# Lambda-layer kernel: one q load moved to ScalarE's queue, weight slots interleaved with the last output tiles, loads of the next x tied to TensorE's slots

## The chip, the cores and the metric

One core of one Trainium2 chip. The metric is the device time of one launch in microseconds, for a batch of 32 images. Less is better.

## The reference

For each of 32 images (512 channels, 64 x 64 pixels, float32), with n = group normalization of x over 32 groups:

```
h   = relu(bn1(conv1x1(n, w1)))                     # 512 -> 128 channels
q   = bnq(conv1x1(h, q_w))                          # 4 heads x 16
k   = softmax over the 16 of conv1x1(h, k_w)
v   = bnv(conv1x1(h, v_w))                          # 32 channels
content = k v^T over all pixels                     # 16 x 32
pos     = conv 15x15 of v with emb (16 kernels)     # 16 x 32 per pixel
out = q . (content + pos)                           # 4 heads x 32 = 128
out = bn3(conv1x1(relu(bn2(out)), w3))              # 128 -> 512
result = x + relu(out + n)
```

## The kernel before

**Tiling.** An image is 4 chunks (j) of 1024 pixels. X holds a chunk as 128 partitions x 4 channel tiles (t) x 1024. The 16 output tiles are called oj.t, tile number 4j + t. PSUM is a ring of four tiles of 128 x 1024 (ring 0 to 3); each named step of TensorE takes one, by a fixed table (`placed`), and waits until the step that had it before has been moved out.

**Stages of an image.** The loop over images has two stages on every engine, and each engine runs through its own list in order.

- `lam(b)`: the position part of image b. The 15 x 15 window is treated as six units u. For each unit TensorE first makes eight weight slots w{u}.{s} (L508: q times the expanded emb, 4 matmuls of 256 columns), which ScalarE or VectorE copy from the ring to `region` (L702; the table BY_DVE says which are VectorE's), and then multiplies them with windows of v (L653). The slots run one unit ahead: while unit u is multiplied, w{u+1}.* are made. At units 0 and 3 a content product (L607) starts the sums in rings 2 and 3; the sums of units 0 to 2 are copied out to S (L711) before the content product of unit 3 may begin. Units 1 and 4 add a small rest (L617). In the same stage VectorE takes the group statistics of the next image's x (L884, 32 instructions, four to each half chunk), placed between its slots by STATS_AT: chunk 0 in unit 1 from slot 4 on, ten statistics in unit 2 of which the last two are of chunk 2, the rest in unit 3. The mean and variance products (L545, L547) follow in unit 4.
- mixed stage, order list MIX: conv1 (c0 to c3, L527), q and k/v (L534, L539) of image b + 1, the content sums (cl, L555; cp, L559), the 16 output tiles of image b (L583), and the slots of unit 0 of image b + 1 with the rest r0, r1 (L517). Of the output tiles nine go VectorE (L1031, into one of four buffers T), ScalarE (relu, L741), GpSimd (addition into X, L1189); the other seven are VectorE's alone in two instructions (L1035, L1038). bcur, rcur and r1cur, which these use, are overwritten by VectorE at the end of the stage.

**Where the data goes.** SP issues nearly all transfers, in order: q's parts go to DRAM and come back in another layout (store_q, load_q: L353, L354, L360, six DMAs of 128 KB to a chunk), v likewise as windows (store_v L367, L370; load_v L377, L378, 3 x 1024 KB; load_v3 L384, 672 + 336 KB into the place of the first, once unit 0 is done). store_out is L402 (512 KB each), load_x L345 (2048 KB a chunk, after all stores out of that chunk of X are done), shuffle L389 and L393 (the sums to DRAM and back as h2). ScalarE issues the reload of x for the residual (L788), one chunk after each conv1.

SP's order in a loop step: load_x 0 to 3, load_v3, the two shuffles, then q chunk 0, stores 0 and 1, q chunk 1, store 2, q chunk 2's store, store 3, q chunk 3's store, load_q 2, load_q 3, store_v, stores 4 to 7, load_v, stores 8 to 15. TensorE waits for all four q_in before w0.0.

The order at the end of MIX before:

```
... cl o2.0 cp o2.1 o2.2 o2.3 o3.0 w0.0 o3.1 w0.1 o3.2 w0.2 o3.3 w0.3 w0.4 w0.5 w0.6 w0.7 r0 r1
```

Of the kernel before, what the change touches and what calls it, by code (L numbers as in the profile page):

```python
# [17 lines left out]
CHUNK = 1024  # L18
# [4 lines left out]
SPLIT = [(0, 0), (0, 1), (0, 2), (1, 0), (1, 1), (2, 0)]  # L23
NG = len(SPLIT)
# [7 lines left out]
UNITS = 6  # L32
# [3 lines left out]
NS = 8  # L36
GUARD = 8


BY_DVE = {0: (5, 7), 1: (1, 3, 5), 2: (1, 3), 3: (3,), 4: (3,), 5: (1, 3, 5, 7)}  # L40
ACT_SLOTS = [(u, s) for u in range(UNITS) for s in range(NS) if s not in BY_DVE[u]]
DVE_SLOTS = [(u, s) for u in range(UNITS) for s in range(NS) if s in BY_DVE[u]]

STATS_AT = {1: (0, 0, 0, 0, 2, 2, 2, 2), 2: (1, 1, 1, 2, 1, 1, 2, 1), 3: (2, 2, 2, 2, 2, 2, 2, 0)}


VEC_TILES = [0, 2, 3, 6, 9, 12, 15]
POOL_TILES = [n for n in range(16) if n not in VEC_TILES]
NVEC, NPOOL = len(VEC_TILES), len(POOL_TILES)
# [5 lines left out]


def lead_names():
    return [f"w0.{s}" for s in range(NS)] + ["r0", "r1"]


def mix_names():
    order = ["c0", "nb", "c1", "q0", "k0", "o0.0", "o0.1", "c2", "q1", "k1", "o0.2", "o0.3", "c3", "q2", "k2", "q3", "k3",
             "o1.0", "o1.1", "o1.2", "o1.3", "cl", "o2.0", "cp", "o2.1", "o2.2", "o2.3"]
    lead = lead_names()
    for t in range(4):
        order += [f"o3.{t}", lead[t]]
    return order + lead[4:]


def lam_names():  # L70
# [3 lines left out]
def placed(order, first=0):  # L74


    out, n = {}, first
    for name in order:
        if name[0] == "w":
            out[name] = int(name[3:]) % 2  # L80
        elif name[0] == "r":
            out[name] = int(name[1])
        elif name in ("gm", "gv"):
            out[name] = 1
        elif name.startswith("o3"):
            out[name] = 2 + int(name[3:]) % 2
        elif name == "cp":
            out[name] = out["cl"]
        else:
            out[name] = n % 4  # L90
            n += 1
    return out


def lambda_block(nc, x, w1, bn1, wq, bnq, wk, wv, bnv, emb, bn2, w3, bn3, out):
    B, C, H, W = x.shape
    N = H * W
# [3 lines left out]
    DK = wk.shape[0]  # L101
    DV = wv.shape[0]
    HEADS = QC // DK
    KV = DV + DK
    NCH = N // CHUNK
# [15 lines left out]
    with ctx:  # L121
# [3 lines left out]
        def sem(name):  # L125
            return ctx.enter_context(nc.semaphore(name))
# [3 lines left out]
        Qt = sb("Qt", [P, HEADS * N], BF16)  # L130
# [36 lines left out]
        qD = nc.dram_tensor("q_parts", (QC, NPART, N), BF16, kind="Internal").ap()  # L167
# [13 lines left out]
        o1 = 8192  # L181
# [6 lines left out]
        r1 = region[QC:2 * QC, o1 + 6144:o1 + 8192].rearrange("p (u n) -> p u n", u=2)  # L188
# [33 lines left out]
        w_full = sem("w_full")  # L222
# [44 lines left out]
        half_relu = sem("half_relu")  # L267
# [2 lines left out]

        x_in = [sem(f"x_in{j}") for j in range(NCH)]
        res_in = [sem(f"res_in{j}") for j in range(NCH)]
        out_done = [sem(f"out_done{j}") for j in range(NCH)]
        q_out = [sem(f"q_out{j}") for j in range(NCH)]
        q_in = [sem(f"q_in{j}") for j in range(NCH)]
# [44 lines left out]
                holds[at[name]] = name  # L320
            return out

        LAST_LEAD = {0: "r0", 1: "r1"}
        BEFORE_PRO = prior(PRO, AT_PRO, {})
        BEFORE_LAM = prior(LAM, AT_LAM, LAST_LEAD)
        BEFORE_LAM_END = prior(LAM_END, AT_LAM_END, LAST_LEAD)
# [16 lines left out]
        def _(sp):  # L343
            def load_x(im, j):
                sp.dma_start(X[:, j, :, :], xv[im, :, :, j * CHUNK:(j + 1) * CHUNK]).then_inc(x_in[j], 16)  # L345
# [10 lines left out]
            def load_q(im, j):  # L356
                sp.wait_ge(q_out[j], im * 32 + 32)
                for g, (a, _e) in enumerate(SPLIT):
                    dst = bass.AP(Qt, g * (HEADS * N) + j * CHUNK, [[NG * HEADS * N, DK], [N, HEADS], [1, CHUNK]])
                    sp.dma_start(dst, qD[:, a, j * CHUNK:(j + 1) * CHUNK].rearrange("(h k) n -> k h n", k=DK))\  # L360
                        .then_inc(q_in[j], 16)
# [18 lines left out]
            def load_v3(b):  # L380
                sp.wait_ge(first_done, b + 1)
                for p0, n, col in ((0, 84, 18), (84, 42, 4)):
                    src = bass.AP(vD.tensor, col * WROWS * ROW, [[ROW, n], [BLK * WROWS * ROW, NXB], [1, ROW]])
                    sp.dma_start(V[p0:p0 + n, 0, :, :], src).then_inc(v_in[3], 16)  # L384
# [28 lines left out]
            for g in range(NG):  # L413
                dst = bass.AP(region, g * 16384 + emb_at, [[NG * 16384, DK], [1, RR]])
# [14 lines left out]
            for x0 in (0, PAD + W):  # L429
                for a in range(0, WROWS, BLK):  # L430
                    n = min(BLK, WROWS - a)
# [11 lines left out]
            def lam(b, last):  # L443
                if not last:
                    for j in range(NCH):
                        sp.wait_ge(out_done[j], b * (16 * CT) + HEAD)
                        load_x(b + 1, j)
                load_v3(b)
                shuffle(b, 0)
                shuffle(b, 1)  # L450

            with nc.Fori(0, B - 1, engines=OrderedEngineSet([sp.engine]), hint_back_edge=True,
                         head_slot={sp.engine: 0}) as b:
                lam(b, False)
                store_q(b + 1, 0)
                load_q(b + 1, 0)
                store_out(b, 0)
                store_out(b, 1)
                store_q(b + 1, 1)
                load_q(b + 1, 1)  # L460
                store_out(b, 2)
                store_q(b + 1, 2)
                store_out(b, 3)
                store_q(b + 1, 3)
                load_q(b + 1, 2)
                load_q(b + 1, 3)
                store_v(b + 1)
                for n in range(4, 8):
                    store_out(b, n)
                load_v(b + 1)  # L470
                for n in range(8, 16):
                    store_out(b, n)
            e = B - 1
            for j in range(NCH):
# [240 lines left out]
        def _(act):  # L715
# [86 lines left out]
            def lead(name, at, im):  # L802
# [4 lines left out]
                elif (0, int(name[3:])) in ACT_SLOTS:  # L807
                    slot(at[name], im, 0, int(name[3:]))

            def keys_out(at, im):  # L810
                act.wait_ge(cl_full, im + 1)
                nc.scalar.copy(clS, ring[at["cl"]][96:96 + DK, 0:DV]).then_inc(cl_ready, 1)
# [16 lines left out]
            with nc.Fori(0, B - 1, engines=OrderedEngineSet([act.engine]), hint_back_edge=True,  # L829
                         head_slot={act.engine: 0}) as b:  # L830
                lam(b, True)
                late = []
                for name in MIX:
                    if name[0] in "wr":
                        lead(name, AT_MIX, b + 1)
                    elif name == "cl":
                        keys_out(AT_MIX, b + 1)
                    elif name[0] in "cqk" and name[1] in "0123":
                        front(name, AT_MIX, b + 1, True)
                    for n in late:  # L840
                        relu_half(b, n)
                    late = []
                    if name == "c0":
                        bn2_relu(b, 0)
                        bn2_relu(b, 1)
                    if name == "k0":
                        bn2_relu(b, 2)
                        bn2_relu(b, 3)
                    if name[0] == "o" and int(name[1]) * CT + int(name[3:]) in POOL_TILES:
                        late.append(int(name[1]) * CT + int(name[3:]))  # L850
                assert not late
# [8 lines left out]
        def _(dve):  # L860
# [58 lines left out]
            def keep_for_output(chain):  # L919
                chain(nc.vector.tensor_copy(rcur[:, :], rstd[:, :]))  # L920
                chain(nc.vector.tensor_scalar(r1cur[:, :], rstd[:, :], 1.0, None, ALU.add))
                chain(nc.vector.tensor_copy(bcur[:, :], bnew[:, :]))
# [128 lines left out]
            def mixed(chain, order, at, b, im):  # L1051
                for name in order:
                    if name[0] in "wr":
                        lead(name, at, im)
                    elif name[0] == "o":
                        output(chain, name, at, b)
                    elif name == "nb":
                        gn_bias(at, im)
                    elif name == "cp":
                        content(chain, name, at, im)  # L1060
                    elif name[0] in "qk":
                        front(chain, name, at, im)
                        if name == "k3":
                            softmax_sum(chain, im, NCH - 1)
# [9 lines left out]
            g, be, m, v = (par[:, a, :] for a in range(4))  # L1074
# [23 lines left out]
            for i, rows in ((0, R), (1, R - 1)):  # L1098
                dst = Ep[:, i, GUARD + 3 * WROWS:GUARD + (3 + R) * WROWS].rearrange("p (b a) -> p b a", a=WROWS)
# [25 lines left out]
            with nc.Fori(0, B - 1, engines=OrderedEngineSet([dve.engine]), hint_back_edge=True,  # L1125
                         head_slot={dve.engine: 0}) as b:
                chain = Chain(b * LOOP_LINKS + pre)
                lam(chain, b, True)
                mixed(chain, MIX, AT_MIX, b, b + 1)
                keep_for_output(chain)  # L1130
                assert chain.n == LOOP_LINKS, chain.n
            chain = Chain((B - 1) * LOOP_LINKS + pre)
# [116 lines left out]
```

## Time and profile before

| | |
|---|---|
| runs of the kernel before | 4826.49, 4826.06, 4821.62 us, median 4826.06 |
| the profiled execution | 4817.23 us, its span 4815.5 us |
| TensorE busy (matmul) | 4457.8 us, 93% |
| VectorE, ScalarE, GpSimd busy | 2796.9, 2346.0, 967.9 us |
| mean granted clock of TensorE | 0.949 |
| moved by DMA | 1284.17 MB, mean 267 GB/s |

The busy time of an engine says how much it did, not what held the end. In the chain of waits, time goes to what released the next step. A granted clock of 1.00 is 2.4 GHz and 0.50 is 1.2 GHz. The DMA share is the mean busy share of the 16 DMA engines; it can come out a little over 1. All rows of the loop below are of one image, from 1972 to 2119 us, and the begin of the next.

### The profile page before, as it was taken

How to read it: one execution, taken by the hardware profiler on the slowest of the kernel's cores; microseconds unless marked ns; L12 is line 12 of the kernel's file. 1: busy time of each engine (PE TensorE's matmuls, PEld its weight loads, DVE VectorE, ACT ScalarE, POOL GpSimd, SP SyncE). 2: the span in 40 equal slices, each digit the busy share in tenths (PEclk: the TensorE clock that was granted, in tenths of full speed). 3: DMA queues.
4: the chain of work that ended last, by engine and by line, in shares of the span. 5: the costliest groups of instructions: out<-in, count | busy, mean ns of one | idle time of the engine just before them, and what ended most of it. 6: DMA issues, size and time to landing. Idle time of an engine off the chain costs nothing.

```text
span 4815.5 us, 121009 instructions
## 1 busy us (share of the span) xinstructions
PE 4457.8 (93%) x49366; PEld 2717.4 (56%) x49366; DVE 2796.9 (58%) x4631; ACT 2346.0 (49%) x2880; POOL 967.9 (20%) x529
## 2 busy tenths in 40 slices
PE   4899999999999999999999999999999999999997
PEld 2555565655556655555555555555565556555555
DVE  3465555565655665656656556556566565566564
ACT  1455445554545454445544454544455444545453
POOL 0022211122201222202222112222122221112221
PEclk9899999999999999999999999999999999999998
DMA  3689778888778897788887788977888878889877
GB/s 96 214 278 308 239 265 279 275 296 277 249 272 266 282 309 250 254 274 288 281 291 243 265 266 276 307 251 254 272 292 281 288 245 275 270 273 305 263 248 250
DMA packets 537174, 1284.17 MB, mean 267 GB/s; under 512 B 43048, under 2 KB 225324, under 8 KB 528556
## 3 DMA queue, kind: packets, MB, share of 16 engines
q1 hardware_dynamic: 471276, 1017.22, 65.7%
q10 hardware_dynamic: 65472, 260.05, 14.7%
q8 instruction: 416, 6.82, 0.6%
q14 instruction: 10, 0.08, 0.0%
HBM read 844.79 MB, written 432.33 MB: 265 GB/s over the span
## 4 chain that ended last, share of the span: by engine, by line
PE 45%; SPq 18%; DMA 13%; issue 11%; DVE 6%; POOL 4%; ACT 2%; ACTq 0%; POOLq 0%; DVEq 0%
PE ring L527 16%; DMA X<-x_dram 11%; PE ring L653 10%; PE ring L508 7%; SPq L402 5%; PE ring L583 4%; SPq L360 4%; DVE st L884 3%; DMA q_parts<-region 3%; SPq L377 3%; POOL X L1189 2%; PE ring L534 2%; POOL region L1182 2%; SPq L378 2%; PE ring L539 2%
## 5 line engine op out<-in xcount | busy, mean ns | idle before, releaser
L702 ACT COPY region<-ring 126x1024 f32<-126x1024 f32 x1120 | 1102.9, 1016 | 948.0 <-PE ring L508 934.0
L583 PE MATMUL ring<-h,w3T 128*128 128x512 f32 x2048 | 937.7, 601 | 28.6 <-DVE X L1038 15.3
L653 PE MATMUL ring<-region,V 126*32 126x128 f32 x24576 | 889.2, 289 | 42.9 <-issue 42.7
L527 PE MATMUL ring<-X,w1e 128*128 128x512 f32 x2048 | 907.7, 596 | 3.2 <-DVE w1e L910 3.2
L508 PE MATMUL ring<-Qt,Ep 96*126 96x256 bf16 x5120 | 808.3, 298 | 103.9 <-DVE region L702 52.0
L653 PEld LDWEIGHTS ring<-region,V 126*32 126x32 f32 x24576 | 692.0, 116 | 223.3 <-issue 206.8
L702 DVE COPY region<-ring 126x1024 f32<-126x1024 f32 x416 | 507.5, 1220 | 496.6 <-PE ring L508 496.5
L508 PEld LDWEIGHTS ring<-Qt,Ep 96*126 96x126 bf16 x5120 | 598.9, 146 | 323.1 <-issue 139.4
L884 DVE BATCH_NORM_STATS2 st<-X 128x6 f32<-128x512 f32 x1024 | 624.8, 679 | 198.0 <-DMA X<-x_dram 197.9
L527 PEld LDWEIGHTS ring<-X,w1e 128*128 128x128 f32 x2048 | 384.5, 190 | 468.8 <-issue 465.5
L583 PEld LDWEIGHTS ring<-h,w3T 128*128 128x128 f32 x2048 | 370.0, 190 | 410.9 <-issue 371.5
L993 DVE SCALAR_TENSOR_TENSOR region<-ring,pbi,region 64x512 f32<-64x512 f32 x256 | 179.5, 739 | 723.8 <-ACT region L794 722.8
L1182 POOL TENSOR_TENSOR region<-region 64x1024 bf16<-64x1024 f32 x128 | 273.5, 2137 | 1177.6 <-ACT region L798 1177.6
L1189 POOL TENSOR_TENSOR X<-X,S 128x1024 f32<-128x1024 f32 x160 | 377.5, 2359 | 481.9 <-ACT S L741 481.9
L786 ACT ACTIVATE region<-ring,nb 128x1024 f32<-128x1024 f32 x128 | 142.5, 1113 | 625.8 <-PE ring L527 352.2
L1175 POOL MEMSET region<- 64x224 f32 x32 | 9.1, 284 | 2170.4 <-PE ring L653 2126.8
L1035 DVE SCALAR_TENSOR_TENSOR ring<-X,r1cur,ring 128x1024 f32<-128x1024 f32 x224 | 287.2, 1282 | 40.8 <-PE ring L583 40.8
L1189 POOL TENSOR_TENSOR X<-X,region 128x1024 f32<-128x1024 f32 x128 | 302.5, 2363 | 11.8 <-ACT region L741 7.9
L539 PEld LDWEIGHTS ring<-wkvT,region 128*128 128x128 f32 x2048 | 238.2, 191 | 103.8 <-issue 77.9
L1038 DVE SCALAR_TENSOR_TENSOR X<-ring,bcur,X 128x1024 f32<-128x1024 f32 x224 | 287.7, 1284 | 8.0
L741 ACT ACTIVATE S<-S,bcur 128x1024 f32<-128x1024 f32 x160 | 183.5, 1147 | 202.3 <-DVE S L1031 200.9
L539 PE MATMUL ring<-wkvT,region 128*128 128x48 f32 x2048 | 254.1, 277 | 0.0
(130 smaller groups left out, 3317.4 us busy)
## 6 DMA issues: line engine op xcount, KB each, us to landing
X<-x_dram SPq DMA_DIRECT2D x132, 2048.0 KB, 20.1
out_dram<-X SPq DMA_DIRECT2D x512, 512.0 KB, 8.0
X<-x_dram ACTq DMA_DIRECT2D x124, 2048.0 KB, 10.6
Qt<-q_parts SPq DMA_DIRECT2D x768, 128.0 KB, 3.1
V<-v_windows SPq DMA_DIRECT2D x96, 1024.0 KB, 10.5
lambda_sums<-S SPq DMA_DIRECT2D x64, 1024.0 KB, 5.0
h<-lambda_sums SPq DMA_DIRECT2D x256, 256.0 KB, 5.0
q_parts<-region SPq DMA_DIRECT2D x128, 256.0 KB, 4.2
```

The lines of the kernel that those rows point to most:

```text
L402: sp.dma_start(ov[b, :, t, j * CHUNK:(j + 1) * CHUNK], X[:, j, t, :]).then_inc(out_done[j], 16)
L508: last = nc.tensor.matmul(dst[0:TROWS, i * 256:(i + 1) * 256], taps(u, xo, yo), Q[:, :, xo * BLK + yo, :], start=(i % 2 == 0), stop=True, ...
L527: last = nc.tensor.matmul(dst[:, hh * HALF:(hh + 1) * HALF], w1e[:, c, :], X[:, j, c, hh * HALF:(hh + 1) * HALF], start=(c == 0), stop=(c ...
L539: last = nc.tensor.matmul(dst[:, i * KV:(i + 1) * KV], h1[:, j % 2, i * P:(i + 1) * P], wkvT[:, :], start=True, stop=True)
L583: last = nc.tensor.matmul(dst[:, yb * HALF:(yb + 1) * HALF], w3T[:, t, :], src, start=True, stop=True)
L653: last = nc.tensor.matmul(bank_of(i)[c * DV:(c + 1) * DV, (g % 4) * P:(g % 4 + 1) * P], V[0:TROWS, VSLOT[t], xb, yb * DV:(yb + 1) * DV], W ...
L702: return engine_copy(dst, src)
L884: return nc.vector.bn_stats(st[:, c, 2 * j + hh, :], X[:, j, c, hh * HALF:(hh + 1) * HALF])
L1035: nc.vector.scalar_tensor_tensor(src[:, :], X[:, j, t, :], r1cur[:, t:t + 1], src[:, :], ALU.mult, ALU.add).then_inc(whole_sum, 1)
L1038: nc.vector.scalar_tensor_tensor(X[:, j, t, :], src[:, :], bcur[:, t:t + 1], X[:, j, t, :], ALU.add, ALU.max).then_inc(out_ready, 1)
L1182: nc.gpsimd.tensor_tensor(q12[:, 1, cols], r1[:, j % 2, :], q12[:, 0, cols], ALU.subtract)\
L1189: nc.gpsimd.tensor_tensor(X[:, j, t, :], X[:, j, t, :], T[i % 4], ALU.add).then_inc(pool_out, 1)
```

## The change

- The last q chunk's six loads move from SP to ScalarE's queue, behind its copy of the content sums `cl`. ScalarE waits there for q_out[3].
- MIX is reordered: slots w0.0 and w0.1 go behind o2.2 and o2.3, and two steps (w0.2 and w0.3; r0 and r1; w0.4 and w0.5; w0.6 and w0.7) go behind each of o3.0 to o3.3. o2.2 and o2.3 take ring 2 and 3. VectorE's slots of unit 0 are 3 and 5 instead of 5 and 7.
- load_x(1), (2) and (3) wait until TensorE has finished 8, 14 and 20 slots of lam (w1.7, w2.5, w3.3). load_v3 stands behind load_x(1) instead of behind load_x(3). x_turn is counted up around the wait and nothing waits for it.
- store_out(7) goes behind load_v.
- VectorE waits for ScalarE's last relu of the image before it overwrites bcur.

The order at the end of MIX after:

```
... cl o2.0 cp o2.1 o2.2 w0.0 o2.3 w0.1 o3.0 w0.2 w0.3 o3.1 r0 r1 o3.2 w0.4 w0.5 o3.3 w0.6 w0.7
```

```diff
-BY_DVE = {0: (5, 7), 1: (1, 3, 5), 2: (1, 3), 3: (3,), 4: (3,), 5: (1, 3, 5, 7)}
+BY_DVE = {0: (3, 5), 1: (1, 3, 5), 2: (1, 3), 3: (3,), 4: (3,), 5: (1, 3, 5, 7)}
+X_AFTER = [0, 8, 14, 20]
 def lead_names():
-    return [f"w0.{s}" for s in range(NS)] + ["r0", "r1"]
+    return ["w0.0", "w0.1", "w0.2", "w0.3", "r0", "r1", "w0.4", "w0.5", "w0.6", "w0.7"]
 def mix_names():
...
-             "o1.0", "o1.1", "o1.2", "o1.3", "cl", "o2.0", "cp", "o2.1", "o2.2", "o2.3"]
-    lead = lead_names()
+             "o1.0", "o1.1", "o1.2", "o1.3", "cl", "o2.0", "cp", "o2.1", "o2.2", "w0.0", "o2.3", "w0.1"]
+    lead = lead_names()[2:]
     for t in range(4):
-        order += [f"o3.{t}", lead[t]]
-    return order + lead[4:]
+        order += [f"o3.{t}", lead[2 * t], lead[2 * t + 1]]
+    return order
...
-        elif name.startswith("o3"):
+        elif name.startswith("o3") or name in ("o2.2", "o2.3"):
             out[name] = 2 + int(name[3:]) % 2
...
-        LAST_LEAD = {0: "r0", 1: "r1"}
+        LAST_LEAD = {0: "w0.6", 1: "w0.7"}
...
                     for j in range(NCH):
                         sp.wait_ge(out_done[j], b * (16 * CT) + HEAD)
+                        if j:
+                            sp.sem_inc(x_turn, 1)
+                            sp.wait_ge(w_full, b * (UNITS * NS) + NS + X_AFTER[j])
+                            sp.sem_inc(x_turn, 1)
                         load_x(b + 1, j)
-                load_v3(b)
+                        if j == 1:
+                            load_v3(b)
+                else:
+                    load_v3(b)
                 shuffle(b, 0)
...
                 load_q(b + 1, 2)
-                load_q(b + 1, 3)
                 store_v(b + 1)
-                for n in range(4, 8):
+                for n in range(4, 7):
                     store_out(b, n)
                 load_v(b + 1)
-                for n in range(8, 16):
+                for n in range(7, 16):
...
+            def load_q(im, j):
+                act.wait_ge(q_out[j], im * 32 + 32)
+                for g, (a, _e) in enumerate(SPLIT):
+                    dst = bass.AP(Qt, g * (HEADS * N) + j * CHUNK, [[NG * HEADS * N, DK], [N, HEADS], [1, CHUNK]])
+                    act.dma_start(dst, qD[:, a, j * CHUNK:(j + 1) * CHUNK].rearrange("(h k) n -> k h n", k=DK))\
+                        .then_inc(q_in[j], 16)
...
                         keys_out(AT_MIX, b + 1)
+                        load_q(b + 1, NCH - 1)
...
                 mixed(chain, MIX, AT_MIX, b, b + 1)
+                dve.wait_ge(half_relu, b * NPOOL + NPOOL)
                 keep_for_output(chain)
```

## Rows read from the trace of the kernel before

**Rows 1.** The page: busy time of the engines, and DMA queue q1.

```profile
PE 4457.8 (93%) x49366; PEld 2717.4 (56%) x49366; DVE 2796.9 (58%) x4631; ACT 2346.0 (49%) x2880; POOL 967.9 (20%) x529
...
q1 hardware_dynamic: 471276, 1017.22, 65.7%
```

**Rows 2.** The chain that ended last: start us, us, what.

```profile
1972.03 7.06 PE ring L527 x16
...
2065.52 19.62 DMA X<-x_dram
...
2119.18 7.06 PE ring L527 x16
```

**Rows 3.** Timeline of TensorE: start us, us, instruction, count [idle before <-releaser].

```profile
2049.64 0.65 PE L508 MATMUL ring<-Qt,Ep 96*126 96x256 bf16 x4 [0.67 <-ACT region L702]
...
2053.91 1.03 PE L517 MATMUL ring<-Qt,E 96*22 96x256 bf16 x4 [0.78 <-DVE region L702]
...
2057.30 3.60 PE L607 MATMUL ring<-Qt,CLp 96*32 96x512 bf16 x16
...
2077.72 0.36 PE L617 MATMUL ring<-Qt 22*32 22x16 f32 x20 [1.21 <-issue]
...
2088.22 0.65 PE L508 MATMUL ring<-Qt,Ep 96*126 96x256 bf16 x4 [1.09 <-DVE region L702]
...
2093.66 1.90 PE L607 MATMUL ring<-Qt,CLp 96*32 96x512 bf16 x16 [0.53 <-DVE S L711]
```

**Rows 4.** Timeline of VectorE: the statistics in lam, then tile 9's last step.

```profile
2080.09 4.84 DVE L884 BATCH_NORM_STATS2 st<-X 128x6 f32<-128x512 f32 x8 [5.96 <-DMA X<-x_dram]
2085.17 1.88 DVE L884 BATCH_NORM_STATS2 st<-X 128x6 f32<-128x512 f32 x3 [0.23 <-DMA X<-x_dram]
...
2091.05 1.87 DVE L884 BATCH_NORM_STATS2 st<-X 128x6 f32<-128x512 f32 x3
...
2184.87 1.28 DVE L1038 SCALAR_TENSOR_TENSOR X<-ring,bcur,X 128x1024 f32<-128x1024 f32 x1
```

**Rows 5.** Windows: stretch, length, busy by engine (count), PEclk, DMA share, GB/s.

```profile
2030.00:2045.00 15.00, 14.49 (x92) 7.55 (x89) 14.75 (x17) 8.31 (x9) 12.91 (x6) 1.00 0.79 201
2045.00:2062.00 17.00, 14.28 (x91) 7.58 (x93) 9.28 (x11) 9.71 (x10) 5.83 (x3) 0.74 1.03 338
2092.00:2097.00 5.00, 4.47 (x62) 2.76 (x62) 5.00 (x9) 2.75 (x4) 0.00 (x0) 1.00 1.04 231
2049.00:2054.00 5.00, 2.58 (x17) 1.61 (x18) 4.07 (x4) 3.36 (x4) 2.04 (x1) 0.92 1.01 326
2053.50:2063.50 10.00, 9.31 (x65) 5.00 (x66) 3.32 (x6) 3.17 (x4) 0.00 (x0) 0.50 1.07 354
```

**Rows 6.** Timeline of SP's queue: issue of q loads 2 and 3, and of V3.

```profile
2030.13 7.61 SPq L360 DMA_DIRECT2D Qt<-q_parts  x12
...
2076.09 13.17 SPq L384 DMA_DIRECT2D V<-v_windows  x2
```

**Rows 7.** ScalarE's copy of the keys; tile Qt, 2170 to 2200: q loads and landing.

```profile
2178.83 0.18 ACT L812 COPY Qt<-ring 16x32 f32<-16x32 f32 x1
2181.36 1.15 ACT L741 ACTIVATE region<-region,bcur 128x1024 f32<-128x1024 f32 x1 [2.36 <-DVE region L1031]
...
L360 SPq DMA_DIRECT2D Qt<-q_parts x12: 593/596/601, 2177.9 to 2185.0; - x12
...
DMA to landing us min/median/max: 2.6/2.7/2.8
```

**Rows 8.** Loads of x2 and x3: SP's issue; KB each, us to landing.

```profile
2068.63 1.50 SPq L345 DMA_DIRECT2D X<-x_dram  x1
...
X<-x_dram SPq DMA_DIRECT2D x1, 2048.0 KB, 21.6
...
2074.33 1.72 SPq L345 DMA_DIRECT2D X<-x_dram  x1
...
X<-x_dram SPq DMA_DIRECT2D x1, 2048.0 KB, 23.2
```

More of the change, by code:

```diff
@@ L272, in lambda_block @@
         res_in = [sem(f"res_in{j}") for j in range(NCH)]
+        x_turn = sem("x_turn")
         out_done = [sem(f"out_done{j}") for j in range(NCH)]
```

## Prediction

> **What bounds the kernel now.** I read the page first. TensorE is busy for 93% of the span, so TensorE looks like the bound, but the queue q1, which SP feeds, alone takes 65.7% of the time of all 16 DMA engines [rows 1]. Next I read the chain that ended last over one image. The first conv1 block of two images in a row starts at 1972.03 and 2119.18, 147.15 us apart, and the loop does this 31 times. Inside the image the chain doesn't stay on TensorE. It runs through SP's issue of X chunk 0, a DMA wait of 19.62 us, the statistics on VectorE, VectorE's copy of the sums, and comes to TensorE only at its second content product, at 2093.66 [rows 2, 3].
>
> TensorE's own timeline of that image shows where it idles. There are gaps of 0.67 to 0.78 us at the end of the mixed stage (from w0.5 to r1, the first and the last of four shown, some 2.5 us together). One of 1.21 us is labelled issue, which means that it waited for nothing the profile shows. There are 1.09 us at slot w3.5, whose ring is held by w3.3, a VectorE slot, and 0.53 us in front of the content product [rows 3]. VectorE shows why the last two exist. It sat 5.96 us until chunk 0 landed at 2080.09 and again until chunk 1 landed at 2085.17. The copy of w3.3 stands behind three statistics of chunk 1 in its program, and the copy of the last sums behind two statistics of chunk 2 [rows 4].
>
> The windows tell what sets the landing of x. From 2045 on the DMA engines are full (share 1.03, and 1.04 still at 2092 to 2097), from 2030 to 2045 they are not (0.79). The clock granted to TensorE is 0.50 from 2053.5 to 2063.5, that is 1.2 instead of 2.4 GHz, after a stretch with 2.58 us of work in 5.00 [rows 5]. So two paths meet at 2088 to 2094: TensorE's own work, and SP, then DMA, then statistics. The second ends last, by about 1.6 us.
>
> **Part 1, q chunk 3 on ScalarE's queue.** SP issued chunks 2 and 3 together, 12 DMAs in 7.61 us, and store_v starts only after them, at 2037.8 [rows 6]. Six of them leave: 3.8 us less in front of store_v, the stores, load_v and the next x. SP's gain is the DMA engines' only as far as they had room. In 2030 to 2045 the room is 15 x (1.03 - 0.79) = 3.6 us [rows 5]. ScalarE can't use the first 2 us or more: its copy of the keys, behind which the load stands, starts at 2178.83 in the next image [rows 7], which is 147.15 us earlier, at 2031.7, in this one. So I take 2.8 us; bounds 1.0 (the two queues only share) and 3.8 (all of SP's time).
>
> The Trainium skill, "DMA: Bandwidth & Descriptors", section "Issuing engines are not separate DMA queues", says that starting DMAs from several engines saves only the sequencer's time, as all run on the same 16. By that rule nothing beyond SP's own issue time could be won, and the share of 1.03 agrees that a full stretch gives nothing.
>
> On ScalarE the six cost the same 3.8 us (593 to 601 ns each) and stand ahead of the relu of tile 7, which started at 2181.36 after 2.36 us of idling [rows 7]. It moves to about 2183.3, GpSimd's addition of that tile with it. VectorE needs that addition only at its fourth-next T buffer, and store 7 now stands behind load_v; so nothing. The last q load is issued about 2182.7 and lands 2.7 later [rows 7], at 2185.4; slot w0.0 now wants it at 2184.4. The conv3 behind it waits for its ring until VectorE has tile 9, 2186.15 [rows 4], so this wait costs nothing, and without that cover 1 us.
>
> **Part 2, two slots behind each of the last tiles.** The work is the same; the order changes. Before, three VectorE copies (w0.5, w0.7, r1) stood alone at the end and each held TensorE. Now all but the last two slots lie between conv3 tiles, rings 2 and 3 serve o2.2 to o3.3, and the last VectorE work is tile 15. I laid the order out with 1.78 us a conv3 tile, 0.45 a slot, 1.2 a VectorE copy or sum and 1.0 a ScalarE copy. VectorE waits about 0.8 and 1.0 us for o2.3 and o3.0 and is then nearly continuous, done with tile 15 at 2054.4. Content then starts at 2054.9 instead of 2057.30 [rows 3]: 2.4 us. The clock may stay at 1.0, too. Half clock makes the content product 3.60 us instead of 1.90 [rows 3]; over the 10 us at 0.50, with 9.31 us of work that would take little over half [rows 5], some 4 us. TensorE so wins 2.4 to 6.5 us here. But this is the path that does not end last: it just reaches w3.5 earlier and waits longer. I book 0.
>
> **Part 3, loads of x held apart.** load_x(1) waits for w1.7, load_x(2) for w2.5, load_x(3) for w3.3, and load_v3 stands behind load_x(1). In the new order TensorE reaches these at about 2063 to 2066, 2070 to 2073 and 2080 to 2083. SP's queue already blocks it about as long: the last of the four x issues ended at 2076.09 and V3 kept SP for 13.17 us more [rows 6]. So I expect the waits to cost nothing by themselves. What changes is the order of the data: V3 (1008 KB) goes ahead of x2 and x3 instead of behind them.
>
> Its price isn't in the trace, as it never stood there. Lower bound: 1008 KB at 338 GB/s, the rate of the stretch with the other V loads, 3.0 us [rows 5]. Upper bound: x2 landed at 2068.63 + 21.6 = 2090.2, x3 at 2074.33 + 23.2 = 2097.5 [rows 8]. These are 7.3 us apart where x1 and x2 are 5.0 apart, and in this interval V3's transfer ran beside it at 231 GB/s [rows 5]. So a load that V3 mixes with loses up to 2.3 more, 5.3 in all. I take 4.1.
>
> The Trainium skill, same page, section "Why a DMA increments its semaphore by 16 and not by 1", has a rule against this part: the number of engines must divide the outermost sizes, so V3's 84 and 42 rows use 14 of 16. By it the 3.0 would be an estimated 3.4 us; no row here shows engines singly.
>
> **Sum for an image.** x2 lands at 2090.2 - 2.8 + 4.1 = 2091.5. Its first statistic ran at 2091.05 + 0.62 = 2091.7 [rows 4], so the content product comes 0.2 us earlier. VectorE reaches that point at 2088.9 and idles 2.6 us on chunk 2. TensorE's wait of 1.6 us in front of the content product becomes 1.6 - 0.2 + (2.4 to 6.5) = 3.8 to 7.9 us. That is as thin a stretch as the one with 2.58 of 5.00 busy, after which the clock fell [rows 5]. If the clock is low behind the content product, where TensorE has no slack, it costs up to 3.4 us; nothing if the low stretch ends under the wait. I take 1.0 us, that is less than a third of it. Sum: -0.2 + 1.0 = +0.8 us, times 31 = +25 us. The last image has no next x, and the new wait of VectorE for half_relu is over when it comes (ScalarE's last relu about 2051.8, tile 15 later): both nothing. The profiled execution took 4817.2 us, 8.8 below the median of the runs, which lie from 4821.6 to 4826.5. Against it the sum is 4842, against the median 4851; I say 4846. A difference under 0.2% (9.7 us, 0.31 us an image) can't be told from none.
>
> **Rivals.**
> - *The SP chain wins* (0.34). V3 costs its lower bound and SP's time counts in full: x2 lands at 2090.2 - 3.8 + 3.0 = 2089.4, 2.3 us earlier than needed before, x 31 = -71 us: 4755. If V3 finds room that delays nothing, -3.8 x 31 = -118: 4708. For it: the engines' room before 2045. Against it: they are full afterwards, and V3 can't be hidden in a full stretch.
> - *Nothing moves* (0.18). -0.2 stands and the clock costs nothing or is repaid by fewer issue gaps, which fall into the wait: 4817 to 4835.
> - *The low clock moves* (0.06). Both stalls together bring 1.2 GHz to the second content product of every image, +3.4, and V3 costs its upper bound with 2.0 us won on SP: 2093.5, +1.8. Sum +5.2, 161 us: 4985. [...]
> - *The holding does nothing* is part of all: if the slot waits are always past when SP reaches them, the three waits could be taken out without effect; only V3's place counts. If instead x1 waited for w1.7 with an empty queue, every microsecond of it would be in x2.
>
> **How the numbers follow.** Likeliest (0.42): slower, +0.3 to +2.5 us an image, 4836 to 4900, at 4846. The range reaches to both neighbours: down to 4745 (all of the first rival but its tail), up to 4925 (+3.4 an image). Faster 0.34, same 0.18, slower 0.48.
>
> **What would show it.** SP: store_v starts 3.8 us sooner after the q stores. x0 lands 2.8 us sooner after the last q store, x2 lands 13 to 16 us after x0 instead of 10. VectorE idles on X twice in lam, now also before the second sums. TensorE has the four gaps at the end of the mixed stage gone, and longer ones at w3.5 and before the content product; the 0.50 stretch moves from the first to behind those. The prediction is wrong if x2 lands before VectorE wants it, if TensorE's waits in front of the content product don't grow, or if x chunk 0 comes much more than 3 us sooner.

## The result, and the profile after

The changed kernel takes 4976.49 us (median of 4 runs, 4970.6 to 4984.04), the kernel before 4823.84 beside it: ratio 1.032, 95% interval 1.0301 to 1.034. It is slower, as forecast, but by 153 us and not by 20 or 25, and outside the range. That is 4.9 us in each of the 31 loop steps instead of 0.8.

The page of the changed kernel, busy times and the two DMA queues (lines have moved: L508 is L518, L583 is L593, L607 is L617, L653 is L663, L617 is L627, L517 is L527, L702 is L712, L884 is L902, L345 is L349, L384 is L388):

```profile
PE 4405.1 (89%) x49366; PEld 2703.1 (54%) x49366; DVE 2798.1 (56%) x4631; ACT 2334.4 (47%) x2880; POOL 968.2 (19%) x529
...
q1 hardware_dynamic: 456396, 992.83, 62.6%
q10 hardware_dynamic: 80352, 284.45, 15.9%
```

Against [rows 1] TensorE is busy 53 us less. The loss is waiting. The view of waits names it (engine, line, who was waited for, us in total, times, longest):

```profile
PE ring L518 <- DMA Qt<-q_parts: 214.6, 32, 8.7
...
PE ring L663 <- issue: 143.3, 33, 6.1
...
DVE st L902 <- DMA X<-x_dram: 89.0, 40, 4.9
...
SPq L454 <- PE ring L518: 676.1, 92, 15.2
```

TensorE waits 6.7 us an image for the last q chunk, and stands still 4.3 us at a time in the products of unit 1 or 2, labelled issue. Before, these were 8.2 us in all (once, ahead of the loop) and 42.7 us in all. SP is held 7.3 us at a time by the new waits, so they do bind. The timeline of TensorE in one image shows both, where [rows 3] had the gaps of 0.67 to 0.78, 1.21 and 1.09. Of the four at the end of the mixed stage 0.70, 0.67 and 0.26 are left:

```profile
2110.52 1.11 PE L518 MATMUL ring<-Qt,Ep 96*126 96x256 bf16 x4 [6.93 <-DMA Qt<-q_parts]
2120.86 0.61 PE L527 MATMUL ring<-Qt,E 96*22 96x256 bf16 x4 [0.70 <-DVE region L712]
2127.51 0.65 PE L518 MATMUL ring<-Qt,Ep 96*126 96x256 bf16 x4 [0.67 <-ACT region L712]
...
2146.72 0.36 PE L627 MATMUL ring<-Qt 22*32 22x16 f32 x20 [1.44 <-issue]
2156.17 0.65 PE L663 MATMUL ring<-region,V 126*32 126x128 f32 x7 [2.70 <-issue]
2166.74 1.90 PE L617 MATMUL ring<-Qt,CLp 96*32 96x512 bf16 x16
```

The second content product, at 2166.74, has no wait in front of it: in this kernel TensorE waits 0.5 us in all for VectorE's slots and 0.3 for its sums. The chain that ended last agrees. In nearly every image it comes to TensorE over the last q load and then stays there:

```profile
2101.75 8.54 DMA Qt<-q_parts
2110.52 1.11 PE ring L518 x4
...
2145.28 1.44 issue
...
2153.46 2.70 issue
```

The gap of 2.70 isn't new, it is longer. It falls inside the 32 products of one step, behind the 25th, where kernel.py has no wait; so it is a wait neither for x nor for V3. In the images before and after this one it is 4.47 and 4.75. The kernel before has it behind the 26th, and [rows 3] leaves it out:

```profile
2084.11 0.42 PE L653 MATMUL ring<-region,V 126*32 126x128 f32 x6 [1.62 <-issue]
```

The loads behind the wait for q, tile Qt from 2093 to 2112 (to be read beside [rows 7]), and the stretches in which V3 is under way (beside [rows 5]):

```profile
L824 ACTq DMA_DIRECT2D Qt<-q_parts x6: 602/670/2122, 2098.1 to 2101.7; - x6
...
DMA to landing us min/median/max: 2.8/4.0/8.5
```

```profile
2138.00:2144.00 6.00, 6.00 (x156) 4.78 (x156) 3.06 (x4) 2.77 (x4) 0.00 (x0) 1.00 1.02 407
2144.00:2151.00 7.00, 5.56 (x143) 4.64 (x143) 4.23 (x8) 3.49 (x4) 0.00 (x0) 0.84 1.06 241
2151.00:2157.00 6.00, 3.30 (x37) 2.23 (x37) 1.88 (x3) 1.93 (x2) 0.00 (x0) 0.50 1.03 253
```

The last q load lands 8.5 us after its issue instead of 2.7. And once V3's rows are in the queue the rate falls from 407 to 241 GB/s with the DMA engines as full as before. VectorE's statistics and SP's issue of x2 (beside [rows 4, 8]) give the landings:

```profile
2143.38 4.85 DVE L902 BATCH_NORM_STATS2 st<-X 128x6 f32<-128x512 f32 x8 [0.48 <-DMA X<-x_dram]
2151.02 1.88 DVE L902 BATCH_NORM_STATS2 st<-X 128x6 f32<-128x512 f32 x3 [2.79 <-DMA X<-x_dram]
```

```profile
2144.26 1.33 SPq L349 DMA_DIRECT2D X<-x_dram  x1
...
X<-x_dram SPq DMA_DIRECT2D x1, 2048.0 KB, 17.1
```

x0 is there at about 2143.4, x1 at 2151.0, x2 at 2144.26 + 17.1 = 2161.4: 7.6 and 10.4 us apart, 18 in all, where it was 10.1. Counted from the first conv1 of the image (2038.19, before 1972.03), x0 comes 2.9 us sooner and x2 5.0 later. VectorE's first statistic of x2 runs at 2163.5 (2162.87 + 0.62), so x2 is there 2.1 us early. The path over x isn't far behind, and in the image before this one, whose gap is 4.47, the chain does go over x2 (its landing, 19.48 us, is the only one of x among the longest pieces of the chain).

### The profile page after: what moved, and what is told of

It reads as the page before. It is cut to its first block, busy times and chain, and to the rows that moved or that the text cites. A ratio compares the mean times of both kernels' runs of the same rounds, so it can differ in the third digit from the quotient of the medians.

```text
span 4975.0 us, 121288 instructions
## 1 busy us (share of the span) xinstructions
PE 4405.1 (89%) x49366; PEld 2703.1 (54%) x49366; DVE 2798.1 (56%) x4631; ACT 2334.4 (47%) x2880; POOL 968.2 (19%) x529
## 3 DMA queue, kind: packets, MB, share of 16 engines
q8 instruction: 416, 6.82, 0.6%
## 4 chain that ended last, share of the span: by engine, by line
PE 71%; issue 7%; ACT 6%; DMA 6%; DVE 6%; ACTq 2%; SPq 1%; POOL 0%; DVEq 0%; POOLq 0%
PE ring L537 18%; PE ring L663 15%; PE ring L518 15%; PE ring L593 10%; DMA Qt<-q_parts 5%; PE ring L544 4%; PE ring L549 2%; PE ring L617 2%; ACTq L824 2%; PE ring L627 2%; ACT region L804 2%; DVE region L1011 1%; ACT region L808 1%; ACT region L712 1%; DVE ring L1053 1%
## 5 line engine op out<-in xcount | busy, mean ns | idle before, releaser
L712 ACT COPY region<-ring 126x1024 f32<-126x1024 f32 x1120 | 1104.3, 1016 | 1113.1 <-PE ring L518 1104.8
L518 PE MATMUL ring<-Qt,Ep 96*126 96x256 bf16 x5120 | 800.9, 299 | 256.9 <-DMA Qt<-q_parts 214.6
L593 PE MATMUL ring<-h,w3T 128*128 128x512 f32 x2048 | 1003.9, 631 | 13.4 <-ACT h L731 13.4
L663 PE MATMUL ring<-region,V 126*32 126x128 f32 x24576 | 862.4, 284 | 143.4 <-issue 143.3
L518 PEld LDWEIGHTS ring<-Qt,Ep 96*126 96x126 bf16 x5120 | 610.0, 148 | 488.0 <-issue 398.1
L663 PEld LDWEIGHTS ring<-region,V 126*32 126x32 f32 x24576 | 670.4, 114 | 299.3 <-issue 292.4
L712 DVE COPY region<-ring 126x1024 f32<-126x1024 f32 x416 | 507.0, 1219 | 565.0 <-PE ring L518 542.0
L902 DVE BATCH_NORM_STATS2 st<-X 128x6 f32<-128x512 f32 x1024 | 624.6, 678 | 89.1 <-DMA X<-x_dram 89.0
L593 PEld LDWEIGHTS ring<-h,w3T 128*128 128x128 f32 x2048 | 383.8, 201 | 387.9 <-issue 353.8
L1049 DVE SCALAR_TENSOR_TENSOR region<-X,rcur,ring 128x1024 f32<-128x1024 f32 x128 | 163.0, 1273 | 260.6 <-PE ring L593 260.6
```

What stands on the lines that cost most here:

```text
L518: last = nc.tensor.matmul(dst[0:TROWS, i * 256:(i + 1) * 256], taps(u, xo, yo), Q[:, :, xo * BLK + yo, :], start=(i % 2 == 0), stop=True, ...
L593: last = nc.tensor.matmul(dst[:, yb * HALF:(yb + 1) * HALF], w3T[:, t, :], src, start=True, stop=True)
L663: last = nc.tensor.matmul(bank_of(i)[c * DV:(c + 1) * DV, (g % 4) * P:(g % 4 + 1) * P], V[0:TROWS, VSLOT[t], xb, yb * DV:(yb + 1) * DV], W ...
L712: return engine_copy(dst, src)
L902: return nc.vector.bn_stats(st[:, c, 2 * j + hh, :], X[:, j, c, hh * HALF:(hh + 1) * HALF])
```

## The experiments

Ratios are to the kernel before, run beside each on the same chip, with 95% intervals.

**First four: one part alone, or one part undone.** My first theory after the result was that the q loads make the loss. The four edits, in short:

```diff
 # e1: the changed kernel
-                        load_q(b + 1, NCH - 1)        # ScalarE, behind keys_out
                 load_q(b + 1, 2)
+                load_q(b + 1, 3)                      # SP, ahead of store_v
 # e2: the kernel before, with the reverse of that (and store 7 behind load_v)
 # e3: the kernel before, with the new lead_names, mix_names, rings, BY_DVE[0], half_relu wait
 # e4: the kernel before, with the three waits and V3 behind load_x(1)
```

> The changed kernel with the six loads of q chunk 3 back on SP's queue, in front of store_v; all else as changed. Theory 1 (the loss is made by those loads: on ScalarE's queue they land some 8 us after their issue, because SP's v stores go out beside them, and slot w0.0 waits 6.7 us an image): the wait of w0.0 falls under 3 us, the time to 4800 to 4850. Rival (the loss is made by the place of V3 and the waits between the loads of x, which leave TensorE a gap of 4.7 us in unit 1): the gap stays and the time stays above 4930. Both at work: 4870 to 4920.

> The kernel before with nothing but the six loads on ScalarE's queue (and store 7 behind load_v). Theory 1: w0.0 comes only behind o3.0 here, 3.7 us later than in the changed kernel, so it waits about 3 us an image: 4890 to 4930. Rival: SP is 3.8 us earlier and nothing is lost: 4740 to 4826.

> The kernel before with nothing but the new order of the slots and output tiles. Theory 1: w0.0 waits about 2 us for q chunk 3 on SP, of which VectorE covers 1.7; the gaps at the end of the mixed stage shrink, and TensorE waits for x instead: 4800 to 4830. Rival (the order itself costs, as nothing may follow w0.0 until q is there): 4860 or more.

> The kernel before with nothing but the waits between the loads of x and V3 behind x chunk 1. Theory 1: x2 lands 3.0 to 5.3 us later and VectorE has 1.5 us to spare, so 1.5 to 3.8 us an image: 4870 to 4945. Rival (all of the loss is here): 4960 to 4990 and the gap of 4.7 us in unit 1 is there.

| | median us | ratio | interval |
|---|---|---|---|
| e1, parts 2 and 3 | 5025.67 | 1.0449 | 1.0421 to 1.0476 |
| e2, part 1 alone | 4883.68 | 1.0152 | 1.012 to 1.0183 |
| e3, part 2 alone | 4825.81 | 1.0041 | 1.0025 to 1.0058 |
| e4, part 3 alone | 5025.42 | 1.0436 | 1.0405 to 1.0468 |

The theory fell: without the q loads on ScalarE's queue the time isn't 4800 to 4850 but 1.3% above the changed kernel (ratios 1.0449 and 1.032). Most of the loss is in part 3; e1 and e4 are above even the 4990 that I had allowed for all of it. Part 1 costs 1.5% by itself and gives 1.3% back beside part 3. In e4 the gap labelled issue stays small (33.5 us in all), and the loss stands as TensorE's waits for VectorE (112.4 and 106.3 us), which waits for x. In the changed kernel TensorE, held back by q, has no such waits, and the stretch of slow transfer costs it longer issue gaps instead.

e3 answers whether TensorE's saving at the end of the mixed stage is worth anything. Its TensorE timeline shows a new wait for q and the wait at w3.5, 1.09 in [rows 3], grown instead:

```profile
2055.17 0.65 PE L508 MATMUL ring<-Qt,Ep 96*126 96x256 bf16 x4 [1.69 <-DMA Qt<-q_parts]
...
2102.60 0.65 PE L508 MATMUL ring<-Qt,Ep 96*126 96x256 bf16 x4 [4.01 <-DVE region L702]
```

**Next four: what of part 3, and why the q loads are late.**

```diff
 # e7: the kernel before; V3 behind x chunk 1, no waits
                         load_x(b + 1, j)
-                load_v3(b)
+                        if j == 1:
+                            load_v3(b)
 # e8: the kernel before; the three waits, V3 behind x chunk 3 as it was
 # e9: the changed kernel without part 3
 # e5: the changed kernel
                 load_q(b + 1, 2)
+                sp.wait_ge(q_in[3], (b + 1) * (16 * NG) + 16 * NG)
                 store_v(b + 1)
```

> The kernel before with V3's loads behind x chunk 1 and no wait between the loads of x. If the place of V3 makes the loss of 4.4% that part 3 has by itself (x1 slowed by 2 to 3 us, x2 another 5.6 us behind V3 before its own 5): x2 lands 18 to 19 us after x0 and the time is 4980 to 5040. Rival (the waits make it, SP issuing x2 late): x2 lands 13 to 15 us after x0, 4810 to 4880.

> The kernel before with the three waits for TensorE's slots and V3 behind x chunk 3 as before. If only V3's place counts: SP's queue holds SP as long as the waits do, 4800 to 4830. Rival (the waits leave the DMA engines without x): x2 and x3 land 2 us or more later than before, 4870 or more.

> The changed kernel without part 3: loads of x and V3 as before. q chunk 3 on ScalarE's queue still lands at 71.7 us of the image instead of 67.6, and slot w0.0 is wanted at 65: a wait of 6.7 us. If this wait is a loss only as far as the path over x has no slack to hide it: x0 lands 3 us earlier, TensorE's content product starts 5.7 us later than before, so TensorE's path is the last one and the time is 4900 to 4960. Rival (x still ends last, the wait is hidden): under 4830.

> The changed kernel with one wait more: SP issues store_v only when q chunk 3 has landed, so that no v store runs beside ScalarE's q loads. If it is the v stores beside them that make these loads slow (last landing 8.5 us after the last issue): they land 3 to 4 us after it, near 67 us of the image, and slot w0.0's wait falls from 6.7 to 2 us; v, the stores and x are 3 us later again, so the time stays 4970 to 5040. Rival (ScalarE's queue is slow by itself): the landing stays at 71 to 72.

| | median us | ratio | interval |
|---|---|---|---|
| e7, V3's place alone | 5025.02 | 1.0434 | 1.0411 to 1.0457 |
| e8, the waits alone | 4824.49 | 1.0011 | 0.9994 to 1.0028 |
| e9, parts 1 and 2 | 4854.44 | 1.0077 | 1.0051 to 1.0102 |
| e5, v stores behind the q loads | 5067.2 | 1.053 | 1.0501 to 1.056 |

V3's place is the whole of part 3 by itself (e7 and e4 are 1.0434 and 1.0436); the waits alone change nothing. In e7 VectorE's statistics wait for each of the three chunks, and TensorE for VectorE, 5.91 and 2.64 us, where [rows 3] had 1.09 and 0.53:

```profile
2163.20 4.84 DVE L891 BATCH_NORM_STATS2 st<-X 128x6 f32<-128x512 f32 x8 [6.80 <-DMA X<-x_dram]
2172.12 1.88 DVE L891 BATCH_NORM_STATS2 st<-X 128x6 f32<-128x512 f32 x3 [4.08 <-DMA X<-x_dram]
...
2182.75 1.29 DVE L891 BATCH_NORM_STATS2 st<-X 128x6 f32<-128x512 f32 x2 [4.06 <-DMA X<-x_dram]
```

```profile
2175.18 1.11 PE L515 MATMUL ring<-Qt,Ep 96*126 96x256 bf16 x4 [5.91 <-DVE region L709]
...
2184.78 1.90 PE L614 MATMUL ring<-Qt,CLp 96*32 96x512 bf16 x16 [2.64 <-DVE S L718]
```

x2 is 19.6 us behind x0, 9.5 more than before, for a load of 1008 KB. The windows of that image show the rate behind it. The engines are full and move less than half:

```profile
2158.00:2162.00 4.00, 2.92 (x92) 2.40 (x84) 0.00 (x0) 2.22 (x4) 0.00 (x0) 1.00 1.01 413
2166.00:2170.00 4.00, 3.03 (x50) 2.22 (x50) 2.04 (x4) 1.70 (x2) 0.00 (x0) 1.00 1.08 172
2170.00:2174.00 4.00, 0.00 (x0) 0.00 (x0) 1.88 (x4) 0.81 (x2) 0.00 (x0) 0.92 1.11 198
```

e5 lands the last q loads 4.2 us after their issue instead of 8.5, and TensorE's wait for them falls from 6.93 to 2.17 us, so it is mostly SP's v stores beside them that make them late, not ScalarE's queue. Its time is worse, 27 us above the 5040 that I had allowed: the v stores and all behind them are later, and TensorE waits for VectorE, and VectorE for x (538.9 us), as in e1:

```profile
L825 ACTq DMA_DIRECT2D Qt<-q_parts x6: 602/617/726, 2136.3 to 2139.6; - x6
...
DMA to landing us min/median/max: 2.6/3.4/4.2
```

e9 waits for q as long as the changed kernel (220.6 us in all) and no longer for x (18.7 us, against 197.9 before): with part 1 the two paths change places, and TensorE's own is the last one. At 4854 it lies between my 4900 to 4960 and the rival's 4830: the wait for q is mostly paid for by the waits for VectorE that it replaces and by TensorE's shorter busy time (4367.0 us, 4457.8 before).

e9 and the changed kernel differ by part 3 alone, 2.4% by their ratios. The views of both show where that stands: the issue gaps in L653's products are 143.3 instead of 48.8 us, TensorE's busy time is 4405.1 instead of 4367.0, and the wait for q is the same.

**V3's shape.** Which rows V3 is made of is the only edit here; base is e7.

```diff
-                for p0, n, col in ((0, 84, 18), (84, 42, 4)):
+                for p0, n, col in ((0, 128, 15),):     # e12; e14: 126 rows; e15: 112 rows
```

> V3's place alone (behind x chunk 1, no waits), but V3 is one load of 128 rows from one column instead of two of 84 and 42 rows from two; 1024 KB instead of 1008. It leaves out the two columns of v that rows 84 to 125 need, so these taps work on other columns of v; no work of the engines changes. If the slow transfer is a matter of V3's shape (84 and 42 rows beside a load of x): the rate beside it stays above 330 GB/s instead of 183 to 206, x2 lands 13 to 14 us after x0, 4830 to 4900. Rival (any load of 1 KB rows in this place is that slow): x2 lands 18 to 19 us after x0, 5000 to 5040.

> V3's place alone (behind x chunk 1, no waits), V3 one load of 126 rows from one column (1008 KB); it leaves out the two columns that rows 84 to 125 need. 126 divides by 14, not by 16. If the number of engines makes V3 slow: like the two loads of 84 and 42 rows, 4980 to 5040, x2 18 to 19 us after x0. If it is that there are two loads, or 6 and 3 rows to an engine: 4815 to 4850.

> The same with 112 rows (896 KB): 16 engines, but 7 rows each instead of 8. It leaves out rows 112 to 125 as well. If the number of engines makes V3 slow: fast, 4810 to 4840. If it is that an engine's share isn't 8 rows: slow, 4950 to 5040.

> The whole changed kernel with V3 in four loads of 80, 4, 32 and 10 rows (16, 4, 16 and 10 engines by their divisors; 5, 1, 2 and 1 rows to an engine) and nothing left out. If the number of engines is it: x2 14 us after x0, and the rest is as parts 1 and 2 alone: 4840 to 4870. If the 8 rows are it: no better, 4960 to 5000.

| | median us | ratio | interval |
|---|---|---|---|
| e12, 128 rows | 4825.74 | 1.0006 | 0.9994 to 1.0018 |
| e14, 126 rows | 4999.35 | 1.0375 | 1.0338 to 1.0411 |
| e15, 112 rows | 4926.1 | 1.024 | 1.0211 to 1.0268 |
| e16, changed kernel, V3 in 80, 4, 32, 10 | 4974.49 | 1.0337 | 1.0311 to 1.0362 |

Two rows fewer than 128 cost 3.7% (ratios 1.0375 and 1.0006). In e12 the stretch with V3 under way keeps its rate, and x2 lands 13.2 us after x0 (2093.50 and 2080.26), 3.1 more than before. That was my lower bound to a tenth. The time doesn't rise with it: TensorE waits 43.5 us in all for the sums instead of 11.0, but its issue gaps in the products that are L617 and L653 before are 71.8 instead of 107.6; why they shrink isn't shown. Windows of e12, of e14 and of e15:

```profile
2081.00:2085.00 4.00, 2.38 (x42) 1.74 (x40) 4.00 (x7) 1.93 (x2) 0.00 (x0) 1.00 1.05 384
2085.00:2089.00 4.00, 2.93 (x48) 2.22 (x46) 3.67 (x7) 2.51 (x3) 0.00 (x0) 1.00 1.07 391
```

```profile
2158.00:2162.00 4.00, 3.01 (x44) 2.40 (x42) 0.31 (x1) 1.97 (x3) 0.00 (x0) 0.87 1.10 178
```

```profile
2132.00:2136.00 4.00, 3.96 (x60) 2.96 (x51) 1.51 (x3) 1.01 (x2) 0.00 (x0) 0.75 1.10 205
2136.00:2140.00 4.00, 0.53 (x4) 0.41 (x4) 3.59 (x6) 1.50 (x2) 0.00 (x0) 1.00 1.04 241
```

By the rule that I had cited (the Trainium skill, "DMA: Bandwidth & Descriptors", section "Why a DMA increments its semaphore by 16 and not by 1") 126 rows go over 14 engines and 112 over all 16. No row shows engines singly, but the number of them isn't the reason alone: 112 rows are slow as well, though less so (1.024, between my two ranges, where 126 rows have 1.0375). e16, with its 80 and 32 rows over 16 by that rule but 4 and 10 rows over fewer, is as slow as the changed kernel. What is left, as an inference, is that only 128 rows have eight rows to each of 16 engines, like the loads of x beside them. The trace doesn't show in what part of the chip they then get in each other's way. Loads of 64 or 96 rows, and the changed kernel with V3 in 128 rows, weren't run.

**A version with the loads of x ahead.** If x ends last, chunks 0 and 1 can be asked for sooner: their places in X are free once stores 0 to 7 are out.

```diff
 # e10: the kernel before
                 load_v(b + 1)
+                for j in range(2):                    # not in the last step
+                    sp.wait_ge(out_done[j], (b + 1) * (16 * CT) + HEAD)
+                    load_x(b + 2, j)
                 for n in range(8, 16):
 # e13: and STATS_AT[2] all 1, STATS_AT[3] all 2
 # e11: and part 2 of the change
 # e17: and V3 in four pieces at its old place, BY_DVE[5] = (3, 5, 7)
```

> The kernel before with chunks 0 and 1 of the next x but one asked for in front of stores 8 to 15 instead of behind them (their places in X are free once stores 0 to 7 are out); V3 last, no slot waits. If the path over x ends last: x0 and x1 land 10 us earlier, the wait at w3.5 goes, the second content product still waits for two statistics of chunk 2, whose landing doesn't move; 4770 to 4810. Rival (the path over x isn't the last one): 4815 to 4830.

> As the one with x ahead, and the two statistics of chunk 2 in unit 2 move to unit 3, behind VectorE's copy of the sums. If the second content product waits for these two: both waits go, 1.6 us an image and more where it was longer; 4750 to 4790. Rival: no different from x ahead alone.

> As the one before, with the new order of slots and output tiles (part 2 of the change). Alone this order brought nothing (1.004), as I read it because TensorE only came sooner to its waits for x. With x ahead the 2 to 3 us that it saves must show: 30 to 90 us less than the same with the old order, 4670 to 4750. Rival (the order has no gain of its own, or x3 takes over as the last landing): within 15 us of the old order.

> The kernel before with the new order of slots, x chunks 0 and 1 ahead of stores 8 to 15, two statistics moved from unit 2 to 3, slot w5.1 given to ScalarE and V3 in four pieces at its old place. If TensorE's wait of 1.6 us at unit 5 in the earlier such kernel came of VectorE's 16 statistics in unit 3 and the late x3: 4720 to 4800. Rival (each gap closed only moves the stretch at half clock): 4820 to 4860.

| | median us | ratio | interval |
|---|---|---|---|
| e10 | 4867.36 | 1.008 | 1.0055 to 1.0105 |
| e13 | 4848.61 | 1.0053 | 1.0034 to 1.0073 |
| e11 | 4865.05 | 1.0097 | 1.0059 to 1.0135 |
| e17 | 4778.59 | 0.993 | 0.9905 to 0.9955 |

The expectations of a gain in e10, e13 and e11 all missed; e17's range was hit. The waits for x are gone or short, as meant (VectorE waits 30.9, 15.3 and 62.7 us in all for X, against 197.9), but the time is no less. e10 and e13 have more of TensorE's issue gaps in the same products (130.4 and 129.7 us, 107.6 before) and a lower mean clock in the profile (0.938 and 0.943, 0.949 before); what makes these isn't shown. In e11, whose profile is of its fastest execution, a new gap stands at unit 5, where VectorE holds a slot, as I read it behind its sixteen statistics of unit 3, and a stretch with the clock at a mean of 0.63 follows:

```profile
2120.85 0.65 PE L519 MATMUL ring<-Qt,E 96*126 96x256 bf16 x4 [1.64 <-DVE region L713]
```

```profile
2120.00:2134.00 14.00, 13.15 (x268) 10.96 (x272) 7.46 (x22) 2.58 (x5) 0.00 (x0) 0.63 0.34 77
```

e17 gives VectorE's first slot of unit 5 to ScalarE and cuts V3, and is the one version here faster than the kernel before, by 0.7%; its mean clock is 0.966 instead of 0.949. Which of its two edits did it wasn't tried apart. V3's pieces did nothing in e16, which speaks for the slot.

## Why the prediction was wrong

**The step that failed first is V3's price in part 3.** I wrote that a load that V3 mixes with loses up to 2.3 more, "5.3 in all", and took 4.1. In e7 it is 9.5 (x2 19.6 us behind x0), in the changed kernel 7.9. The upper bound was built wrongly. I took x3's delay, 7.3 against 5.0, as the whole loss of mixing and let V3's own time be 3.0 us at the rate of the other V loads. But the row that I used for it, 231 GB/s at a share of 1.04 [rows 5], said that the engines were full and moved little more than half, and V3 itself was running in that stretch, on past x3. An estimate from this row alone would have been 1008 KB and 2048 KB at 231 GB/s, 13.5 us for V3 and one x, 8.4 more than x alone; that is nearly what was measured.

**The path was wrong as well.** The sum lets V3's price reach the time through x2 and the second content product only. So it does in e7, e4 and e1. In the changed kernel that product has no wait in front of it, or 0.3 us once. There the price, 2.4% between e9 and the changed kernel, stands in TensorE's issue gaps, 3.0 us an image more, and in a longer busy time, 1.2 us more. The sum has no term for the gaps, and 1.0 us of clock for the busy time. As x2 is only 2.1 us early, shorter gaps alone would win no more than about that (an estimate) before x ends last again. That the slow transfer makes the gaps long is argued from e9 against the changed kernel and from e16; what TensorE waits for in them stays open.

The other step of part 3 was right: the place matters and the waits cost nothing (e8), though not because SP was busy as long anyway: it is held 7 us at a time, and the data still come in time.

**The 14 engines.** I weighed the rule at 3.0 to 3.4 us. The 126 and 112 rows show that shape decides, but by far more than a seventh: the rate is 178 and 205 GB/s where 128 rows have 384.

**Part 1 was half right.** x0 was to come 2.8 us sooner, and comes 2.9 sooner. With part 1 and V3 at its old place (e2, e9) VectorE hardly waits for x any more. The failing lines are "lands 2.7 later [rows 7]" and "so this wait costs nothing": that latency was read where these loads had the queue to themselves, and the move puts SP's v stores beside them. It is 8.5, and the cover of 1.7 us by VectorE's tile 9 is far too short: 6.7 us of wait for an image, in the changed kernel and in e9, 3.2 in e2. e5 shows the cause. The sum took TensorE's own path for the one that doesn't end last, and this wait makes it the last. Where x ends last the wait hides in part, so part 1 gains 1.3% beside part 3 (e1 against the changed kernel); without part 3 it costs 1.5% with the old order (e2) and 0.4% with the new one (e9 against e3).

**Part 2 was nearly right.** I booked 0 because this path doesn't end last. Alone it is +0.4%, which is little but more than the 0.2% that I called none (1.0025 to 1.0058), and its wait at w3.5 goes from 1.09 to 4.01. It also has a wait for q of 1.69 us that the prediction had only for part 1.

**The clock** moves, but not to the place that I gave it. In the changed kernel it is at a mean of 0.55 behind the wait for q, and at 0.50 from 2149 on, which is after the gap of 1.44 us and before the long one, until 2162:

```profile
2110.50:2115.00 4.50, 4.48 (x11) 2.44 (x12) 0.01 (x1) 2.06 (x2) 1.20 (x1) 0.55 0.88 290
...
2149.00:2151.00 2.00, 2.00 (x46) 1.66 (x39) 0.00 (x0) 0.63 (x1) 0.00 (x0) 0.50 1.15 204
```

In e3 it moves too. My 1.0 us for it can't be told from the rest.

**Rivals.** The one that gave nearly this time (4985, at 0.06) got it from the clock and from 2.0 us won on SP with V3 at its upper bound; the time fits by luck, the mechanism is V3's rate, q's landing and TensorE's longer gaps. That SP's chain wins came to nothing: x0 is sooner, but x2 behind V3 is later.

## What to carry to other kernels

Price a transfer that is moved in a full queue by the rate of the stretch in which it now runs, with everything that runs beside it, and not by the rate of loads of the same size elsewhere: full engines with a low rate were here the sign of a load that slows its neighbours in both places. A load moved to a second queue isn't free of the first; ask what the first queue sends in the same microseconds, and who needs the load. And when waits on one path are closed, look at the gaps and the clock that come in their place: in e10, e11 and e13 they took back more than was won.

## What the runs showed of the hardware

- A load of 126 or 112 rows of 1 KB pieces, or two of 84 and 42, beside loads of 128 rows brings the rate from 413 down to 172 to 253 GB/s with the DMA share still 1.03 to 1.11. One of 128 rows keeps it at 384 to 391. Two rows made 3.7% of the kernel's time.
- The last of six q loads of 128 KB on ScalarE's queue lands 8.5 us after issue with v stores on SP's queue beside it, 4.2 without.
- TensorE's gaps labelled issue stand at the same products in each of three images, before and after, one of them inside a run of 32 without a wait in the program, and are longer in the changed kernel, where the transfer is slow: 143.3 us against 42.7 before and 48.8 in e9 on the same products. In queue q8, of kind instruction (416 packets, 6.82 MB), one packet is counted between 2153.5 and 2154.0, in the gap from 2153.46 to 2156.17. Nothing here shows that TensorE waited for it.
- The stretch at 0.50 (1.2 GHz) isn't tied to a place in the program. Before, it begins at 2053.5, after 2.58 us of work in 5.00; in the changed kernel at 2149, after a gap of 1.44 us, with the clock also low right behind the wait of 6.93 us for q.
